# Pre-LN decoder layer with cross-attention and experts on one core: value products taken in pairs every second step, with three probability buffers

## The reference

```python
scores = einsum('bhqd,bhkd->bhqk', q, k) / sqrt(8) + bias[:, None, None, :]
probs  = softmax(scores, axis=-1)          # 16 heads x 56 queries x 1500 keys per batch
out    = einsum('bhqk,bhkd->bhqd', probs, v)
```

## Time and profile before

| | |
|---|---|
| median of 3 runs | 643.82 us |
| span of the profiled execution, first to last instruction | 640.8 us |
| median less span | 3.0 us |
| instructions in the span | 18136 |
| busy: TensorE / VectorE / ScalarE / GpSimd | 89% / 71% / 53% / 25% |
| mean granted TensorE clock | 0.928 of 2.4 GHz |

### The profile page before, as it was taken

The page is one execution under the profiler, slowest core; times in us unless marked ns, Lnnn a source line. Parts: engine busy times, 40 slices in busy tenths (PEclk is TensorE's granted clock), DMA queues, the critical chain, the costliest instruction groups (busy, mean ns, idle before and its releaser), DMA issues.

```text
span 640.8 us, 18136 instructions
## 1 busy us (share of the span) xinstructions
PE 569.6 (89%) x6656; PEld 368.7 (58%) x6656; DVE 458.0 (71%) x879; ACT 342.0 (53%) x509; POOL 162.4 (25%) x105
## 2 busy tenths in 40 slices
PE   3588887588999997999979999799999999689996
PEld 2267665344676774767747677476776666334442
DVE  6954435977888784787747878488788873478885
ACT  2630654314666663666636666366666668235553
POOL 6895000400033033030330303303030004025540
PEclk9975999775999997999969999799999999789999
DMA  4473300143432432224322243222421304002200
GB/s 108 151 143 111 77 0 2 35 103 72 106 79 72 120 77 73 68 68 122 78 70 62 74 116 78 76 57 79 116 79 26 74 2 101 1 13 50 49 0 29
DMA packets 45473, 45.12 MB, mean 70 GB/s; under 512 B 30387, under 2 KB 37259, under 8 KB 45403
## 3 DMA queue, kind: packets, MB, share of 16 engines
q1 hardware_dynamic: 45403, 44.07, 26.2%
HBM read 16.82 MB, written 0.46 MB: 27 GB/s over the span
## 4 chain that ended last, share of the span: by engine, by line
PE 75%; DVE 8%; issue 6%; POOL 5%; DMA 2%; ACT 2%; SPq 1%; ACTq 0%; DVEq 0%; POOLq 0%
PE ps L866 16%; PE ps L767 12%; PE ps L910 11%; PE ps L339 6%; PE ps L340 5%; PE ps L341 5%; PE ps L672 4%; PE ps L975 3%; PE ps L770 3%; PE ps L777 2%; PE ps L729 2%; DVE mx L1506 2%; DMA ctx<-in_ctx 2%; PE ps L960 1%; DVE xn L1252 1%
## 5 line engine op out<-in xcount | busy, mean ns | idle before, releaser
L1506 DVE TENSOR_REDUCE mx<-ps 112x1 f32<-112x500 f32 x384 | 251.0, 673 | 54.3 <-PE ps L866 52.3
L1171 ACT ACTIVATE p<-ps,bres 125x896 f32<-125x896 f32 x192 | 193.1, 1006 | 92.7 <-PE ps L910 91.9
L866 PE MATMUL ps<-ks,qsb 97*112 97x500 f16 x384 | 160.4, 420 | 11.4 <-DVE mx L1506 10.9
L555 POOL TENSOR_TENSOR ch<-ctx,zero 128x1536 f16<-128x1536 f32 x16 | 43.9, 2745 | 286.2 <-DMA ctx<-in_ctx 286.2
L910 PE MATMUL ps<-qsb,ks 98*125 98x224 f16 x768 | 109.9, 266 | 0.0
L767 PE MATMUL ps<-p,v 125*27 125x168 f32 x1664 | 105.8, 322 | 4.4 <-issue 2.8
L910 PEld LDWEIGHTS ps<-qsb,ks 98*125 98x125 f16 x768 | 83.3, 140 | 14.3 <-issue 2.1
L866 PEld LDWEIGHTS ps<-ks,qsb 97*112 97x112 f16 x384 | 50.6, 132 | 41.5 <-DVE mx L1506 21.5
L767 PEld LDWEIGHTS ps<-p,v 125*27 125x27 f32 x1664 | 31.8, 105 | 59.7 <-issue 53.5
L770 PE MATMUL ps<-p,v 125*9 125x56 f32 x1664 | 60.5, 215 | 0.0
L770 PEld LDWEIGHTS ps<-p,v 125*9 125x9 f32 x1664 | 47.1, 92 | 11.1
(11 more groups left out here) (172 smaller groups left out, 799.9 us busy)
## 6 DMA issues: line engine op xcount, KB each, us to landing
ks<-k SPq DMA_DIRECT2D x192, 93.8 KB
ctx<-in_ctx SPq DMA_DIRECT2D x16, 750.0 KB
ks<-in_L_ffn_W SPq DMA_DIRECT2D x48, 64.0 KB, 2.0
qsb<-qs SPq DMA_DIRECT2D x15, 168.0 KB, 7.7
qs<-late SPq DMA_DIRECT2D x8, 168.0 KB, 4.1
ks<-brow SPq DMA_DIRECT2D x64, 2.9 KB
qs<-late SPq DMA_DIRECT2D x16, 56.0 KB, 2.9
qs<-late SPq DMA_DIRECT2D x8, 112.0 KB, 2.5
```

The lines of the kernel that those rows point to most:

```text
L555: nc.gpsimd.tensor_tensor(ch[n][:, 0], ctx[n][:], zero[:].to_broadcast([128, KT, D]), ALU.add).then_inc(ch_step, 1)
L866: mm(mbank[k % 2][0:112, 0:CH], qsb[n][0:ROWS - 1, 2 * pair:2 * pair + 2].rearrange("p h q -> p (h q)"), ks[n][0:ROWS - 1, pair // 2, CH * ...
L1171: A(p[s % 2][0:KP].rearrange("p (a c) -> p a c", a=2), sbank[s % 2][0:KP, :, 0:448], ACT.Exp, scale=SCALE, bias=bres[:, bass.ds(i, 1), s:s ...
L1506: V.tensor_reduce(mx[:, k // 3, k % 3:k % 3 + 1], mbank[k % 2][0:112, 0:CH], axis=AX.X, op=ALU.max).then_inc(mx_read, 1)
```

## The change

The value products of two neighbouring tiles, s - 3 and s - 2, are done back to back at the start of every odd step; even steps have none. There are three probability buffers, `p[s % 3]`; the third lies in the space of `wnat`, which is free by then. On TensorE the misc use moves behind the scores and the first chunk. On ScalarE the exponential moves ahead of the misc copy; on VectorE both maxima move ahead of it. The copy of the finished output (`osb`) moves from step 0 to step 1. What is computed stays the same, and so does the number of matmuls. `scores` is the block of L904 to L914 as a function of its own, and `misc_use` that of L884 to L903.

```diff
@@ probability buffers
         p = [sb(f"p{n}", [128, H * S], F32) for n in range(2)]
+        p.append(wnat[:].rearrange("p n d -> p (n d)")[:, 0:H * S])
@@ TensorE
-                times_v(v[c % 3][:, t], p[t % 2], KP, t == 0, t == KT - 1)
+                times_v(v[c % 3][:, t], p[t % 3], KP, t == 0, t == KT - 1)
...
             def iteration(r, c):
                 for s in range(KT):
-                    use = MISC[s]
-                    if used(r, c, use):
...
+                    (off0, k0), (off1, k1) = chunks(s)
+                    if s % 2:
+
+                        for t in (s - 3, s - 2):
+                            if live(r, c if t >= 0 else c - 1):
+                                pv_tile(r, c if t >= 0 else c - 1, t % KT)
                     if live(r, c):
...
+                        scores(r, c, s)
                     if live(r, c + off0):
                         max_chunk(r, c, off0, k0)
-                    if s == 0 and live(r, c - 1):
-                        pv_tile(r, c - 1, KT - 1)
-                    if s > 0 and live(r, c):
-                        pv_tile(r, c, s - 1)
+                    misc_use(r, c, s)
                     if live(r, c + off1):
                         max_chunk(r, c, off1, k1)
@@ ScalarE
                 for s in range(KT):
+                    if live(r, c):
+                        tile = B + KT * i + s
+                        act.wait_ge(st_done, tile + 1)
+                        act.wait_ge(pv_done, tile - 2)
+                        A(p[s % 3][0:KP].rearrange("p (a c) -> p a c", a=2), sbank[s % 2][0:KP, :, 0:448],
+                          ACT.Exp, scale=SCALE,
...
+                    if s == 1 and live(r, c - 1):
+                        act.wait_ge(pv_done, B + KT * i)
+                        A(osb[:], obank[:, 0:224], ACT.Copy).then_inc(o_read, 1)
                     use = MISC[s]
...
-                    if live(r, c):
-                        tile = B + KT * i + s
-                        act.wait_ge(st_done, tile + 1)
-                        act.wait_ge(pv_done, tile - 1)
-                        A(p[s % 2][0:KP].rearrange("p (a c) -> p a c", a=2), sbank[s % 2][0:KP, :, 0:448],
...
-                    if s == 0 and live(r, c - 1):
-                        act.wait_ge(pv_done, B + KT * i)
-                        A(osb[:], obank[:, 0:224], ACT.Copy).then_inc(o_read, 1)
@@ VectorE: the loop over the two maxima stands ahead of the misc copy
                 for s in range(KT):
+                    for off, k in chunks(s):
...
+                        dve.wait_ge(mx_psum, NCH * b + k + 1)
...
                     use = MISC[s]
...
-                    for off, k in chunks(s):
...
```

More of the change, by code:

```diff
@@ L879, in pv_tile, with misc_use @@
                     pe.wait_ge(o_read, B + 3 * r + c)
-                times_v(v[c % 3][:, t], p[t % 2], KP, t == 0, t == KT - 1)
+                times_v(v[c % 3][:, t], p[t % 3], KP, t == 0, t == KT - 1)
+            def misc_use(r, c, s):
+                use = MISC[s]
+                if used(r, c, use):
+                    if use[0] in "TKV" and not tail(r, c, use):
+                        prepare[use[0]](r, c + 2, int(use[1]))
+                    else:
+                        pe.wait_ge(misc_read, misc_index(r, c, use))
+                    if tail(r, c, use) == "out":
+                        out_project(1, 0, misc, misc_done)
+                    if tail(r, c, use) == "norm":
+                        transpose_norm(2, 0, 6, misc_done)
+                    if tail(r, c, use) == "logits":
+                        router_logits(0, misc).then_inc(misc_done, 1)
+                    if use == "sel":
+                        pe.wait_ge(o_read, B + 3 * r + c)
+                        pick_heads()
+                    elif use == "tr":
+                        tr(misc[:, 0:128], tok[:], ident[:]).then_inc(misc_done, 1)
+                    elif use == "mt":
+                        pe.wait_ge(mcol_ok, 3 * r + c + 2)
+                        tr(misc[0:8, 0:112], mcol[:], ident[0:112, 0:112]).then_inc(misc_done, 1)
@@ new lines, in scores @@
+            def scores(r, c, s):
+                if s == 0:
+                    pe.wait_ge(mrow_in[c % 3], 16 * (r + c // 3 + 1))
+                pe.wait_ge(exp_done, B + KT * (3 * r + c) + s - 1)
+                for g in range(G):
+                    last = mm(sbank[s % 2][0:KP, g // 2, 224 * (g % 2):224 * (g % 2) + 224],
+                              ks[c % 3][0:ROWS, g, KP * s:KP * s + KP],
+                              qsb[c % 3][0:ROWS, HG * g:HG * g + HG].rearrange("p h q -> p (h q)"),
+                              start=True, stop=True)
+                last.then_inc(st_done, 1)
@@ L915, in iteration @@
-                    (off0, k0), (off1, k1) = chunks(s)
+                    (off0, k0), (off1, k1) = chunks(s)
[3 more added lines that the diff above has]
+                                pv_tile(r, c if t >= 0 else c - 1, t % KT)
+                    if live(r, c):
+                        scores(r, c, s)
                     if live(r, c + off0):
                         max_chunk(r, c, off0, k0)
-                    if s == 0 and live(r, c - 1):
-                        pv_tile(r, c - 1, KT - 1)
@@ L1154, in iteration @@
                 for s in range(KT):
+                    if live(r, c):
[4 more added lines that the diff above has]
+                          ACT.Exp, scale=SCALE,
+                          bias=bres[:, bass.ds(i, 1), s:s + 1].rearrange("p o t -> p (o t)")).then_inc(exp_done, 1)
+                    if s == 1 and live(r, c - 1):
+                        act.wait_ge(pv_done, B + KT * i)
+                        A(osb[:], obank[:, 0:224], ACT.Copy).then_inc(o_read, 1)
                     use = MISC[s]
@@ L1166, in iteration @@
                             A(mrow[:], misc[0:8, 0:112], ACT.Copy, scale=1.0 / BIG).then_inc(misc_read, 1)
-                    if live(r, c):
-                        tile = B + KT * i + s
-                        act.wait_ge(st_done, tile + 1)
-                        act.wait_ge(pv_done, tile - 1)
-                        A(p[s % 2][0:KP].rearrange("p (a c) -> p a c", a=2), sbank[s % 2][0:KP, :, 0:448],
-                          ACT.Exp, scale=SCALE,
-                          bias=bres[:, bass.ds(i, 1), s:s + 1].rearrange("p o t -> p (o t)")).then_inc(exp_done, 1)
-                    if s == 0 and live(r, c - 1):
-                        act.wait_ge(pv_done, B + KT * i)
-                        A(osb[:], obank[:, 0:224], ACT.Copy).then_inc(o_read, 1)
                     if s == 3 and isinstance(r, int) and i == B - 1:
@@ L1473, in iteration @@
                 for s in range(KT):
+                    for off, k in chunks(s):
+                        if not live(r, c + off):
+                            continue
+                        b = i + off
+                        dve.wait_ge(mx_psum, NCH * b + k + 1)
+                        if k == 0 and not (isinstance(r, int) and b == 0):
+                            dve.wait_ge(mcol_ok, b)
+                        V.tensor_reduce(mx[:, k // 3, k % 3:k % 3 + 1], mbank[k % 2][0:112, 0:CH],
+                                        axis=AX.X, op=ALU.max).then_inc(mx_read, 1)
+                        if k == NCH - 1:
+                            dve.wait_ge(mx_read, NCH * (b + 1))
+                            V.tensor_reduce(mcol[:], mx[:], axis=AX.X, op=ALU.max, negate=True).then_inc(mcol_ok, 1)
                     use = MISC[s]
```

## The result

The changed kernel takes **673.57 us** (median of 4 runs, 671.41 to 675.04) against 643.79 before: 1.046 of the time before, 95% interval 1.0436 to 1.0485. The profiled execution has a span of 669.7 us, 28.9 more than before. The forecast was slower, 682 us, range 661 to 704.

A forecast was written before the change was run, and what follows sets the result against it. TensorE's own work and the dependency K, ScalarE, VectorE, T were taken as the bound. +2.65 us for each of 13 batches, less the jumps, plus batches 0, 14 and 15 gave +38.5 on 643.8: 682 us, range 661 to 704.

The forecast's parts named there:

- The sign: Whole kernel: slower by over 0.2%, given 90%; same 3%, faster 7%.
- the row of maxima: First scores of the next batch wait for the DMA from `mrow`: +1.2 us per change of batch, except at three jumps.
- The switches saved: TensorE changes between wide and column-grouped matmuls: 0.25 us saved per product pair, six pairs a batch, -1.50 us.
- the Trainium skill's drain: About 128 array cycles per change of shape, two an estimated 0.11 us a pair; by that the forecast would be 11 us longer.
- The K uses: Before T1, T2 and sel, TensorE stands still 0.98 us for ScalarE's copy and VectorE's subtraction: +2.94 us a batch.
- T, V and sel: No wait behind T, 0.09 us to spare; 0.14 each behind V0 and V2, +0.28 a batch; none behind V1 and sel.
- rival B: At changes of batch the row of maxima lands in time, its DMA behind fewer key copies: 667 us, chance 20%.
- SyncE's key copies: In SyncE's queue, 12 copies take 8.0 us; `mrow` is ready 9.6 us after K2's reading, so its DMA is not held up.
- The batches at the edges: Batches without preparation: batch 0 +3.5 us, batch 14 +3.8, batch 15 +2.7.
- the jumps: At three loop jumps, idling hides the row's wait, -3.6 us; K stalls in half-clock stretches behind them drop out, -2.4.
- A: Before T1, T2 and sel, the bank is emptied within 0.81 us, so stalls are covered: faster, 618 us, chance 7%.
- C: In the batch loop, TensorE's standstills take the clock to 1.2 GHz for a third of it: 760 us, chance 5%.

The follow-up runs named there:

- the run with the exponential first: Fastest follow-up kernel (620.24 us: pairs in odd steps, misc use first, second chunks shifted to the next step), with ScalarE's exponential put ahead of its misc copy: 744.79 us.

## Why the prediction was right

The sign, the mechanism and the places were right; the sum was 8.7 us too high (+38.5 forecast, +29.8 measured), mostly in one term, the row of maxima.

- **The switches saved.** In the order of the change: 0.31 from chunk to pair, 0.40 and 0.50 for the two products, 0.43 from the scores behind it to their chunk instead of 0.39, so 1.04 where I had 1.07, and 0.28 saved per pair instead of 0.25. The unseen seam inside the pair costs nothing (in the chain the second product takes 0.28 where the first takes 0.42). By the Trainium skill's drain (TensorE: Matmul & The Clock Gate, "What happens when you issue a matmul") I had an estimated 0.11; the measurement, 0.28, decides against it as the whole price of two changes of shape. The timeline also has the weight loads of the first product starting only with it (at 321.06, behind 0.23 of idling of the loads), those of the second 0.05 ahead of it (321.41); how much of the price that is, no run separates.
- **The K uses.** Forecast: copy at S + 1.21, subtraction at 1.90, next use at 2.64, standstill 0.98. Measured: 1.21, 1.86, 2.59, 0.93, three times a batch (0.28 more the first time, for `osb`). A K and T pair came to 4.68, forecast 4.76. The runs with the orders undone and with the pair moved show that this is the loop through both engines, and not one of them alone.
- **T, V and sel.** No wait behind T, as forecast. The V waits are there: V1 starts at 329.04, 0.13 after TensorE could have.
- **The row of maxima: the term that was mis-sized.** I took 1.2 us for each of 12 changes of batch, from a landing of about 2.1. It lands in 1.82, the profile's figure for the small copy; the DMA starts at S + 1.46, not 1.6; and TensorE arrives at S + 2.76, not 2.5 (all ahead of batch 12; the wait for V2 and longer handovers are in it). The standstill there is 0.52. In eight of the 12 it is 0.3 to 0.6, in the other four 1.0 to 1.4, together about 9 us against 14.4: some 5 us too much, the largest part of the error. My rival B, which had this wait hidden, forecast 667; the truth lay between. In two batches SyncE's key copies took 9.8 and 10.1 us, and the row was issued 0.5 and 0.8 late behind them, which I had excluded.
- **The batches at the edges.** Counted between the first exponentials of each batch, batches 1 to 13 grew by 22.7 us (forecast 28.5), batch 0 by 0.5 (3.5), batch 14 by 4.4 (3.8), batch 15, up to its last product, by 1.3 (2.7). In batch 0 the pair of steps became 3.41 as forecast (3.37), but only for its second half; in its first half the granted clock is 1.2 GHz in both kernels (up to 158.9 us before, 160.2 after), and a chunk waits for VectorE in both (1.0 and 0.7 us). Smaller errors of both signs are in the sum too: the wait for `osb`, which I had missed, adds 0.28 in most of the 13 batches, while the shorter K stall, the larger saving and the jumps (11.8 us of idling around the three of them against 13.7 before) take off some 6 us. So the sum is nearer than its terms, and that is luck.
- **The rivals.** A needed the bank emptied in 0.81 us; it took 1.74 (S + 0.85 to S + 2.59). C, the clock:

```profile
321.00:337.00 16.00, 14.11 (x220) 10.32 (x219) 11.61 (x21) 9.29 (x13) 2.23 (x1) 1.00 0.33 77
```

Over 321 to 337 us TensorE is busy 14.11 of 16 and the granted clock is 1.00. In batches 1 to 13 of the change it fell at the three jumps alone, so standstills near 1 us every 4.7 us cost no clock there. In batch 14 it did fall, for 6.8 us from 549.3 on, behind a standstill of 1.34 us; the kernel before has no such fall in that batch, and part of the 4.4 us may be this. The Trainium skill's rule on short idling (same page, "A second HAM failure mode: psum-queue depth-cycling") has nothing to explain in batches 1 to 13 of the change, but it describes the run with the exponential first, where standstills of up to 1.7 us went with nine falls. My reading that the trace before shows a fall only behind 3.6 us of idling was too narrow: at 247.7 us it stands behind 2.9.

## What to carry to other kernels

Before an operation is moved, write down for each single-buffered bank the loop that empties it, engine by engine and with what stands ahead of it in each queue, and lay TensorE's work between two uses beside it. Work that is gathered into one place saves switches there and takes the cover away everywhere else; here one change brought both the gain (0.28 us per pair) and the loss (0.9 us behind each K use), and placing the pair and the chunks by the two loops kept the gain alone. Shortening one queue's part of a loop does not shorten the wait while another engine is late anyway, and what it gains may be given back one bank further on. And standstills have a second price: in the batch loop those near 1 us left the clock at 2.4 GHz, those of up to 1.7 us did not always.

## What the runs showed that I had not expected

A second fp32 product behind a first of the same column groups starts 0.40 us after it, and taking the products in pairs is worth 28.7 us in all, 4% of this kernel; the switches that go are a part of that, the wait behind K that the pair covers another. The order of one queue, that of ScalarE, which is busy 56% of the time, moved the whole from 620 to 745 us with the same instructions. And the three loop jumps varied from kernel to kernel in what they cost (2.8 to 4.4 us of idling ahead of the first matmul in the kernels before and after), so two kernels' totals differ from 13 times their plain batch by a few us.
